# Mixture-of-experts stage of a two-layer decoder: the gathered token tile is turned by VectorE in 32x32 blocks instead of by TensorE

## The chip, the cores and the metric

The kernel runs as one program on one core of a Trainium2 chip. A core has five engines that run their own instruction streams and meet only at semaphores: TensorE (PE, matrix multiplies and transposes against an identity matrix), VectorE (DVE), ScalarE (ACT), GpSimd (POOL) and SyncE (SP). The metric is the device time of one execution in microseconds, here the median of three runs. All arithmetic of this kernel is in 32-bit floats.

## The reference

A decoder of two layers over 8 sequences of 256 tokens with 512 features. The part that the change touches is the feed-forward block of the first layer, a mixture of 8 experts of which each token uses two:

```
logits = h @ router_w.T                      # 2048 tokens, 8 experts
vals, idx = lax.top_k(softmax(logits), 2)    # two experts per token
vals = vals / vals.sum(axis=-1, keepdims=True)
for each expert e:                           # gate_up_proj[e] is 704 x 512, down_proj[e] 512 x 352
    gate, up = split(h @ gup.T, 2)           # 352 columns each
    y = silu(gate) * up @ dp.T
    out += combine[:, e] * y
x = layernorm(x + out)
```

Before it stand a differential attention and a long convolution, behind it a causal attention, a cross attention and a shared-key attention, each with its layer norm.

## The kernel before, in words

The program is a row of stages with a barrier between them: `front_stage`, `long_conv_stage`, `middle_stage`, `experts_stage`, `tail_stage`. The middle stage computes the routing and sorts the 4096 (token, expert) pairs into 39 tiles (`TILES`) of 128 slots, so that every tile belongs to one expert. It leaves in SBUF the number of the expert of each tile (`tile_expert`), the token of each slot (`tokens`), all weights of the experts (`gu`, `down`), and the first tile already turned (`xT_first`). It also starts the gathers of tiles 0 and 1 into the two buffers `xg`.

`experts_stage` goes over the tiles. For tile s:

- GpSimd gathers the 128 token rows of 512 features from memory into `xg[s % 2]` (L1604), slots on partitions. It may start once tile s - 2 has been turned (`x_turned`).
- The rows must be turned so that features are on partitions. TensorE does this with 4 transposes of 128x128 into the PSUM tile `xT_ps` (`turn_x`, L1618), and VectorE copies that to the single SBUF buffer `xT` (`take_x`, L1700), which signals `xT_taken`.
- TensorE multiplies: `gate` (4 products of 352 columns, summed in PSUM) and `up` (4 more), both at L1623. Each is preceded by `expert(s)` (L1610), with which TensorE's sequencer reads the number of the expert from SBUF into a register, and by a little register arithmetic for the address of the weights. In the instruction stream the waits of `gate` stand ahead of that read.
- ScalarE applies silu to the gate half (L1674), VectorE multiplies it with the up half (`product`, L1705, into `hid`).
- TensorE turns `hid` (3 transposes, L1642), ScalarE copies it (L1689, L1691), TensorE multiplies with the down weights (`down`, 3 products of 512 columns, L1651), VectorE copies the result to `y` (L1717), and ScalarE's queue stores it (L1678).

The order is written out by hand. TensorE's order in a turn of the loop is gate(s+1), turn hid(s), up(s+1), turn_x(s+2), down(s). VectorE's order is product(s+1), take_x(s+2), copy of y(s). The products of gate and up, the PSUM tile of y, `silu`, `hid` and `xg` have two buffers each; `xT` has one.

In the records a 32-bit product appears as two MATMUL instructions, a 32-bit transpose as one.

Of the kernel before, what the change touches and what calls it, by code (L numbers as in the profile page):

```python
# [13 lines left out]
P = 128  # L14
B = 8
# [3 lines left out]
NC = D // P  # L19
# [183 lines left out]
STRIP = 32  # L203
# [723 lines left out]
E_, HID = 8, 352  # L927
HC = [(0, P), (P, P), (2 * P, HID - 2 * P)]
PICKS = 2
TILES = PICKS * B * NT + E_ - 1  # L930
KB4 = 4 * D * NT
AT_CTX = 0
# [221 lines left out]
def ctx_stores(b):  # L1154

    return sum(2 if n >= EARLY else 1 for n in range(b % 2, b, 2))
# [420 lines left out]
def experts_stage(nc, consts, mid, region, x_in, y_slots, early, early_loaded, w_tail):  # L1577


    with ExitStack() as ctx:  # L1580
        st = Stage(nc, ctx, "moe")
        at = AT_SMALL + 320 + 4 * D
        xT = mid.xT
        hT = region.at("moe_hT", at + 2048, [P, 3, P])
        y = [region.at(f"moe_y{p}", at + 3584 + 2048 * p, [P, D]) for p in range(2)]
        silu = region.at("moe_silu", AT_CTX + 2 * KB4, [P, 2, HID])
        hid = region.at("moe_hid", AT_CTX + 2 * KB4 + 2816, [P, 2, HID])
        xg, wgu, wd, gathered = mid.xg, mid.gu, mid.down, mid.gathered
        gu_ps = st.ps("gu_ps", [P, 2, 2, 512])
        xT_ps = st.ps("xT_ps", [P, 512])  # L1590
        hT_ps = st.ps("hT_ps", [P, 512])
        y_ps = st.ps("y_ps", [P, 2, 512])
        y_stored = mid.y_stored
        sem = {n: st.sem(n) for n in (
            "x_turned", "xT_taken", "gate_ready", "up_ready", "silu_ready", "hid_ready", "h_turned", "hT_taken", "y_ready", "y_taken")}

        with nc.Block() as block:
            @block.gpsimd
            def _(pool):
                for s in range(2, TILES):  # L1600
                    p = s % 2
                    if s > 2:
                        pool.wait_ge(sem["x_turned"], s - 2)
                    pool.indirect_dma_start(out=xg[p][:], out_offset=None, in_=x_in,  # L1604
                                            in_offset=bass.IndirectOffsetOnAxis(ap=mid.tokens[:, s:s + 1], axis=0)).then_inc(gathered[p], 16)

            @block.tensor
            def _(pe):
                def expert(s):
                    return pe.value_load(mid.tile_expert[0:1, s:s + 1], min_val=0, max_val=E_ - 1)  # L1610

                def turn_x(s):
                    p = s % 2
                    pe.wait_ge(gathered[p], 16 * (s // 2) + 16)
                    if s > 1:
                        pe.wait_ge(sem["xT_taken"], s - 1)
                    for c in range(NC):
                        ins = pe.transpose(xT_ps[:, c * P:(c + 1) * P], xg[p][:, c * P:(c + 1) * P], consts["ident"][:])  # L1618
                    ins.then_inc(sem["x_turned"], 1)

                def project(s, h, e):
                    for c in range(NC):
                        ins = pe.matmul(gu_ps[:, s % 2, h, 0:HID], (xT if s else mid.xT_first)[:, c, :], wgu[c][:, e, h * HID:(h + 1) * HID],  # L1623
                                        start=c == 0, stop=c == NC - 1)
                    return ins

                def gate(s):
                    if s:
                        pe.wait_ge(sem["xT_taken"], s)
                    if s >= 2:  # L1630
                        pe.wait_ge(sem["hid_ready"], s - 1)
                    project(s, 0, expert(s)).then_inc(sem["gate_ready"], 1)

                def up(s):
                    project(s, 1, expert(s)).then_inc(sem["up_ready"], 1)

                def turn_hid(s):
                    pe.wait_ge(sem["hid_ready"], s + 1)
                    if s:
                        pe.wait_ge(sem["hT_taken"], s)  # L1640
                    for n, (lo, w) in enumerate(HC):
                        ins = pe.transpose(hT_ps[0:w, n * P:(n + 1) * P], hid[:, s % 2, lo:lo + w], consts["ident"][:])  # L1642
                    ins.then_inc(sem["h_turned"], 1)

                def down(s):
                    e = expert(s)
                    pe.wait_ge(sem["hT_taken"], s + 1)
                    if s >= 2:
                        pe.wait_ge(sem["y_taken"], s - 1)
                    for n, (lo, w) in enumerate(HC):  # L1650
                        ins = pe.matmul(y_ps[:, s % 2, :], hT[0:w, n, :], wd[n][0:w, e, :], start=n == 0, stop=n == 2)  # L1651
                    ins.then_inc(sem["y_ready"], 1)

                pe.wait_ge(mid.first_half, 16 * 7)
                gate(0)
                turn_x(1)
                up(0)
                for s in range(TILES):
                    if s + 1 == HALVES[1][0]:
                        pe.wait_ge(mid.second_half, 16 * 6)  # L1660
                    if s + 1 < TILES:
                        gate(s + 1)
                    turn_hid(s)
                    if s + 1 < TILES:
                        up(s + 1)
                    if s + 2 < TILES:
                        turn_x(s + 2)
                    down(s)

            @block.scalar  # L1670
            def _(act):
                def swish(s):
                    act.wait_ge(sem["gate_ready"], s + 1)
                    act.activation(silu[:, s % 2, :], gu_ps[:, s % 2, 0, 0:HID], ACT.Silu).then_inc(sem["silu_ready"], 1)  # L1674

                def store(s):
                    act.wait_ge(sem["y_taken"], s + 1)
                    act.dma_start(y_slots[s * P:(s + 1) * P, :], y[s % 2][:]).then_inc(y_stored[s % 2], 16)  # L1678

                for p in range(2):  # L1680
                    act.wait_ge(mid.ctx_stored[p], 16 * ctx_stores(B - 2 + p))
                for k in early:
                    act.dma_start(early[k][:], w_tail[k].rearrange("(c p) e -> p c e", p=P)).then_inc(early_loaded[k], 16)
                swish(0)
                for s in range(TILES):
                    if s + 1 < TILES:
                        swish(s + 1)
                    act.wait_ge(sem["h_turned"], s + 1)
                    act.copy(hT[:, 0:2, :], hT_ps[:, 0:2 * P].rearrange("p (k n) -> p k n", n=P))  # L1689
                    w = HC[2][1]  # L1690
                    act.copy(hT[0:w, 2, :], hT_ps[0:w, 2 * P:3 * P]).then_inc(sem["hT_taken"], 1)  # L1691
                    if s:
                        store(s - 1)
                store(TILES - 1)

            @block.vector
            def _(dve):
                def take_x(s):
                    dve.wait_ge(sem["x_turned"], s)
                    dve.tensor_copy(xT[:], xT_ps[:].rearrange("p (c n) -> p c n", n=P)).then_inc(sem["xT_taken"], 1)  # L1700

                def product(s):
                    dve.wait_ge(sem["silu_ready"], s + 1)
                    dve.wait_ge(sem["up_ready"], s + 1)
                    dve.tensor_tensor(hid[:, s % 2, :], gu_ps[:, s % 2, 1, 0:HID], silu[:, s % 2, :], ALU.mult).then_inc(sem["hid_ready"], 1)  # L1705

                take_x(1)
                product(0)
                for s in range(TILES):
                    if s + 1 < TILES:  # L1710
                        product(s + 1)
                    if s + 2 < TILES:
                        take_x(s + 2)
                    dve.wait_ge(sem["y_ready"], s + 1)
                    if s >= 2:
                        dve.wait_ge(y_stored[s % 2], 16 * (s // 2))
                    dve.tensor_copy(y[s % 2][:], y_ps[:, s % 2, :]).then_inc(sem["y_taken"], 1)  # L1717
# [1271 lines left out]
```

## Times and profile before

| what | value |
|---|---|
| median of 3 runs | 2129.55 us (2128.58 to 2134.21) |
| span of the profiled execution, first to last instruction | 2127.3 us |
| the median less that span | 2.25 us |
| PE busy | 2057.7 us, 97% |
| DVE busy | 1128.4 us, 53% |
| ACT busy, POOL busy | 518.8 us, 580.5 us |
| mean granted TensorE clock | 0.992 of full speed |
| experts stage, from its first product to the last product of down | about 860 to 1178 us |

The profiled execution has no time of its own beside its span, so the span stands for it. Busy time is the time in which an engine executed instructions; waiting, register and semaphore instructions are not in it. The rows below use the names PEld for TensorE's weight loads, which overlap its products, and PEldq for instructions of TensorE's sequencer (register reads and arithmetic). A row of the timeline has start, duration, engine, line, operation, output<-inputs, and how often; in brackets the idle time of the engine before it and what ended that. Durations of neighbouring rows on one engine can overlap, so that the distance between starts is what an instruction costs in a row of instructions.

### The profile page before, as it was taken

The page shows a single profiled execution, that of the slowest core. Times are in us where ns is not written, and L with a number is a line of the kernel's source. Part 1 is how long each engine was busy: PE and PEld are TensorE (multiplying, and loading weights), DVE is VectorE, ACT ScalarE, POOL GpSimd, SP SyncE. Part 2 cuts the span into 40 slices and gives each one's busy share as a digit, 9 for nine tenths or more (in the row PEclk, how much of TensorE's full clock was granted, in tenths as well). Part 3 has the DMA queues.
Part 4 walks back from the last instruction along what each step waited for, and adds up shares of the span by engine and source line. Part 5 has one row for each costly group of instructions (what it writes and reads, how often), then busy time and mean ns, then how long its engine had stood idle before and what let it go on. Part 6 is the DMA issues. An engine that isn't in the chain of part 4 may idle for free. (4 is left out here: it accounts for less than half of the span.)

```text
span 2127.3 us, 32323 instructions
## 1 busy us (share of the span) xinstructions
PE 2057.7 (97%) x13439; PEld 1194.6 (56%) x13439; DVE 1128.4 (53%) x1731; ACT 518.8 (24%) x791; POOL 580.5 (27%) x548
## 2 busy tenths in 40 slices
PE   7899999999999999999999999999999999999996
PEld 5444444334444557556566655766666666666664
DVE  2567777567777744122222334364646464736567
ACT  2445555440000121101011122122222222222211
POOL 2222222128999600111110312022222222121122
PEclk9999999999999999999999999999999999999998
DMA  5101111205111147321211602100010101000000
GB/s 161 48 1 55 55 56 45 87 38 210 40 43 44 35 156 277 126 65 65 65 65 55 222 3 99 50 31 21 17 44 1 60 1 41 1 31 12 1 11 21
DMA packets 66237, 130.81 MB, mean 61 GB/s; under 512 B 6480, under 2 KB 19920, under 8 KB 66096
## 3 DMA queue, kind: packets, MB, share of 16 engines
q1 hardware_dynamic: 45968, 77.49, 11.1%
q10 hardware_dynamic: 14448, 32.64, 4.3%
q0 software_dynamic: 5680, 18.62, 3.0%
q8 instruction: 111, 1.82, 0.4%
q14 instruction: 30, 0.25, 0.0%
HBM read 97.40 MB, written 41.81 MB: 65 GB/s over the span
## 5 line engine op out<-in xcount | busy, mean ns | idle before, releaser
L1033 PE MATMUL conv_conv<-kv,toep 128*128 128x512 f32 x576 | 247.6, 592 | 0.3 <-POOL kv L1067 0.3
L2615 DVE RECIPROCAL tail_inv<-tail_ring 128x256 f32<-128x256 f32 x63 | 110.7, 1757 | 188.8 <-PE tail_ring L1935 188.3
L1623 PE MATMUL moe_gu_ps<-gu,xT_tile 128*128 x608 | 192.4, 459 | 0.0
L1033 PEld LDWEIGHTS conv_conv<-kv,toep 128*128 128x128 f32 x576 | 109.4, 190 | 139.0 <-issue 129.6
L1067 POOL TENSOR_TENSOR kv<-vT,cT 128x512 f32<-128x512 f32 x128 | 147.0, 1172 | 15.8 <-PE conv_conv L1033 12.0
L2302 POOL TENSOR_TENSOR tail_rstd_x<-tail_rstd_x,const_minus_half 128x2 f32<-128x2 f32 x31 | 21.8, 702 | 469.6 <-DVE tail_rstd_x L2577 469.6
L1623 PEld LDWEIGHTS moe_gu_ps<-gu,xT_tile 128*128 128x128 f32 x608 | 112.3, 190 | 66.5 <-issue 17.8
L2310 POOL TENSOR_SCALAR_AFFINE_SELECT tail_expT<-tail_expT 128x1024 f32<-128x1024 f32 x64 | 71.5, 1119 | 242.1 <-ACT tail_expT L2394 242.0
L2603 DVE TENSOR_REDUCE tail_negtop<-tail_scores 128x4 f32<-128x1024 f32 x64 | 78.2, 1221 | 95.6 <-PE tail_scores L1886 95.4
L594 POOL TENSOR_SCALAR_AFFINE_SELECT front_expT<-front_expT 128x2048 f32<-128x2048 f32 x32 | 64.3, 2008 | 199.1 <-ACT front_expT L649 199.1
L1604 POOL DMA_INDIRECT xg<-x_after,tokens x37 | 35.0, 947 | 282.3 <-PE moe_xT_ps L1618 255.2
L1705 DVE TENSOR_TENSOR moe_hid<-moe_gu_ps,moe_silu 128x352 f32<-128x352 f32 x39 | 20.5, 525 | 170.7 <-PE moe_gu_ps L1623 170.7
L649 ACT ACTIVATE front_expT<-front_scores 128x2048 f32<-128x2048 f32 x48 | 90.1, 1878 | 78.3 <-PE front_scores L367 78.3
L1651 PE MATMUL moe_y_ps<-down,moe_hT 128*128 (+1 forms) x234 | 107.1, 593 | 0.7 <-ACT moe_hT L1691 0.7
L2394 ACT ACTIVATE tail_expT<-tail_scores 128x1536 f32<-128x1536 f32 x63 | 91.4, 1451 | 64.8 <-PE tail_scores L1912 64.8
L1674 ACT ACTIVATE moe_silu<-moe_gu_ps 128x352 f32<-128x352 f32 x39 | 18.1, 464 | 270.2 <-PE moe_gu_ps L1623 270.2
L770 DVE TENSOR_REDUCE front_negtop<-front_scores 128x8 f32<-128x2048 f32 x32 | 73.2, 2288 | 18.6 <-PE front_scores L335 18.4
L2315 POOL TENSOR_TENSOR tail_expT<-tail_expT 128x512 f32<-128x512 f32 x60 | 76.7, 1279 | 5.0
L1089 ACT COPY both<-conv_conv 128x512 f32<-128x512 f32 x32 | 18.7, 586 | 229.9 <-PE conv_conv L1033 211.0
L1717 DVE COPY moe_y<-moe_y_ps 128x512 f32<-128x512 f32 x39 | 27.0, 692 | 72.7 <-PE moe_y_ps L1651 72.7
L198 PE MATMUL tail_ring<-tail_gk,tail_xT 128*128 128x416 f32 (+1 forms) x256 | 63.4, 399 | 1.5 <-ACT tail_xT L2376 1.5
L1651 PEld LDWEIGHTS moe_y_ps<-down,moe_hT 128*128 128x128 f32 (+1 forms) x234 | 41.6, 191 | 38.5 <-issue 38.3
(394 smaller groups left out, 3912.2 us busy)
## 6 DMA issues: line engine op xcount, KB each, us to landing
toep<-toeplitz SPq DMA_DIRECT2D x32, 320.0 KB, 2.9
y_slots<-moe_y ACTq DMA_DIRECT2D x39, 256.0 KB, 2.0
gu<-in_L_ffn_gate_up_proj SPq DMA_DIRECT2D x5, 1408.0 KB, 12.5
toeplitz<-filt_rows SPq DMA_DIRECT2D x8, 768.0 KB
front_e<-in_ctx SPq DMA_DIRECT2D x8, 512.0 KB, 4.7
toeplitz<-filt_rows SPq DMA_DIRECT2D x16, 256.0 KB
x_after<-x SPq DMA_DIRECT2D x8, 512.0 KB, 5.0
tail_x<-x_after SPq DMA_DIRECT2D x8, 512.0 KB, 3.7
```

The costliest lines, as they stand in the source:

```text
L594: pool.affine_select(out=tile, in_=tile, compare_op=ALU.is_ge, fill=0.0, base=0, pattern=[[0, 16], [1, P]], channel_multiplier=-1).then_in ...
L649: act.activation(exp_buf(b, n)[:].rearrange("p g j q -> p g (j q)"), scores[:], ACT.Exp).then_inc(quads.drained_sem(key), 1)
L770: ins = dve.tensor_reduce(negtop[:, 1, n].rearrange("p (g a) -> p g a", a=2), scores[:].rearrange("p g (a k) -> p g a k", a=2), AX_X, ALU. ...
L1033: ins = pe.matmul(bank, toep[p][:, mat * P:(mat + 1) * P], kv[p][:, c].rearrange("p b j i -> p (b j i)"), start=n == 0, stop=n == len(PART ...
L1067: pool.tensor_tensor(kv[p][:, c], tokens_of(c, h), context_of(c, h, 3), ALU.mult).then_inc(kv_ready, 1)
L1623: ins = pe.matmul(gu_ps[:, s % 2, h, 0:HID], (xT if s else mid.xT_first)[:, c, :], wgu[c][:, e, h * HID:(h + 1) * HID], start=c == 0, stop ...
L1651: ins = pe.matmul(y_ps[:, s % 2, :], hT[0:w, n, :], wd[n][0:w, e, :], start=n == 0, stop=n == 2)
L2310: pool.affine_select(out=diagonal, in_=diagonal, compare_op=ALU.is_ge, fill=0.0, base=0, pattern=[[0, 8], [1, P]], channel_multiplier=-1). ...
L2315: pool.tensor_tensor(e[:, 3], e[:, 0], e[:, 2], ALU.add).then_inc(masked[kind], 1)
L2394: act.activation(exp_buf(kind, b, c)[:, 0:3].rearrange("p n g q -> p g n q"), quads.tile(key)[:, :, 0:3 * P].rearrange("p g (n q) -> p g n ...
L2603: dve.tensor_reduce(negtop[:, 1, heads_of(c)], scores[:, :, 0:S], AX_X, ALU.max, negate=True)
L2615: link.after(dve.reciprocal(inv[c % 2][:], bank[:, S:2 * S]))
```

## The change

The four transposes by TensorE and VectorE's copy out of PSUM are gone, and so are the PSUM tile `xT_ps` and the semaphore `xT_taken`. VectorE now turns the tile itself, SBUF to SBUF. One instruction reads 32 slots (one strip of 32 partitions) by 4 blocks of 32 features and writes 32 features (one strip of partitions) by 4 blocks of 32 slots; 16 of them, for all pairs of strips, make up a tile. The buffer `xT` now has two halves, by the parity of the tile. `x_turned` is raised by the last of the 16, and both `gate(s)` and the gather of tile s + 2 wait for it. From tile 3 on, the turns of tile s wait in addition for `up(s - 2)`, the last reader of the same half. The turns of tile 1, which write to an area that a store of the middle stage still reads, wait for that store (`ctx_stored`).

```diff
@@ -1580,19 +1580,18 @@
     with ExitStack() as ctx:
         st = Stage(nc, ctx, "moe")
         at = AT_SMALL + 320 + 4 * D
-        xT = mid.xT
+        xT = [mid.xT, region.at("moe_xT1", AT_CTX + 2 * KB4 + 5632, [P, NC, P])]
         hT = region.at("moe_hT", at + 2048, [P, 3, P])
         y = [region.at(f"moe_y{p}", at + 3584 + 2048 * p, [P, D]) for p in range(2)]
         silu = region.at("moe_silu", AT_CTX + 2 * KB4, [P, 2, HID])
         hid = region.at("moe_hid", AT_CTX + 2 * KB4 + 2816, [P, 2, HID])
         xg, wgu, wd, gathered = mid.xg, mid.gu, mid.down, mid.gathered
         gu_ps = st.ps("gu_ps", [P, 2, 2, 512])
-        xT_ps = st.ps("xT_ps", [P, 512])
         hT_ps = st.ps("hT_ps", [P, 512])
         y_ps = st.ps("y_ps", [P, 2, 512])
         y_stored = mid.y_stored
         sem = {n: st.sem(n) for n in (
-            "x_turned", "xT_taken", "gate_ready", "up_ready", "silu_ready", "hid_ready", "h_turned", "hT_taken", "y_ready", "y_taken")}
+            "x_turned", "gate_ready", "up_ready", "silu_ready", "hid_ready", "h_turned", "hT_taken", "y_ready", "y_taken")}
 
         with nc.Block() as block:
             @block.gpsimd
@@ -1609,24 +1608,15 @@
                 def expert(s):
                     return pe.value_load(mid.tile_expert[0:1, s:s + 1], min_val=0, max_val=E_ - 1)
 
-                def turn_x(s):
-                    p = s % 2
-                    pe.wait_ge(gathered[p], 16 * (s // 2) + 16)
-                    if s > 1:
-                        pe.wait_ge(sem["xT_taken"], s - 1)
-                    for c in range(NC):
-                        ins = pe.transpose(xT_ps[:, c * P:(c + 1) * P], xg[p][:, c * P:(c + 1) * P], consts["ident"][:])
-                    ins.then_inc(sem["x_turned"], 1)
-
                 def project(s, h, e):
                     for c in range(NC):
-                        ins = pe.matmul(gu_ps[:, s % 2, h, 0:HID], (xT if s else mid.xT_first)[:, c, :], wgu[c][:, e, h * HID:(h + 1) * HID],
+                        ins = pe.matmul(gu_ps[:, s % 2, h, 0:HID], (xT[s % 2] if s else mid.xT_first)[:, c, :], wgu[c][:, e, h * HID:(h + 1) * HID],
                                         start=c == 0, stop=c == NC - 1)
                     return ins
 
                 def gate(s):
                     if s:
-                        pe.wait_ge(sem["xT_taken"], s)
+                        pe.wait_ge(sem["x_turned"], s)
                     if s >= 2:
                         pe.wait_ge(sem["hid_ready"], s - 1)
                     project(s, 0, expert(s)).then_inc(sem["gate_ready"], 1)
@@ -1653,7 +1643,6 @@
 
                 pe.wait_ge(mid.first_half, 16 * 7)
                 gate(0)
-                turn_x(1)
                 up(0)
                 for s in range(TILES):
                     if s + 1 == HALVES[1][0]:
@@ -1663,8 +1652,6 @@
                     turn_hid(s)
                     if s + 1 < TILES:
                         up(s + 1)
-                    if s + 2 < TILES:
-                        turn_x(s + 2)
                     down(s)
 
             @block.scalar
@@ -1695,22 +1682,30 @@
 
             @block.vector
             def _(dve):
-                def take_x(s):
-                    dve.wait_ge(sem["x_turned"], s)
-                    dve.tensor_copy(xT[:], xT_ps[:].rearrange("p (c n) -> p c n", n=P)).then_inc(sem["xT_taken"], 1)
+                def turn_x(s):
+                    dve.wait_ge(gathered[s % 2], 16 * (s // 2) + 16)
+                    if s > 2:
+                        dve.wait_ge(sem["up_ready"], s - 1)
+                    rows = xg[s % 2][:].rearrange("p (c d) -> p c d", d=P)
+                    for a in range(4):
+                        for k in range(4):
+                            lane, tokens = slice(STRIP * k, STRIP * (k + 1)), slice(STRIP * a, STRIP * (a + 1))
+                            ins = dve.transpose(xT[s % 2][lane, :, tokens], rows[tokens, :, lane])
+                    ins.then_inc(sem["x_turned"], 1)
 
                 def product(s):
                     dve.wait_ge(sem["silu_ready"], s + 1)
                     dve.wait_ge(sem["up_ready"], s + 1)
                     dve.tensor_tensor(hid[:, s % 2, :], gu_ps[:, s % 2, 1, 0:HID], silu[:, s % 2, :], ALU.mult).then_inc(sem["hid_ready"], 1)
 
-                take_x(1)
+                dve.wait_ge(mid.ctx_stored[1], 16 * ctx_stores(B - 1))
+                turn_x(1)
                 product(0)
                 for s in range(TILES):
                     if s + 1 < TILES:
                         product(s + 1)
                     if s + 2 < TILES:
-                        take_x(s + 2)
+                        turn_x(s + 2)
                     dve.wait_ge(sem["y_ready"], s + 1)
                     if s >= 2:
                         dve.wait_ge(y_stored[s % 2], 16 * (s // 2))
```

VectorE in two turns of the loop, before and after. `moe_hid` is the product, `xT_tile` and `moe_xT` are the two halves of the turned tile, `moe_y` is the result tile.

```order
L1705 TENSOR_TENSOR moe_hid<-moe_gu_ps,moe_silu 128x352 [waits moe_up_ready,moe_silu_ready]
L1700 COPY xT_tile<-moe_xT_ps 128x512 [waits moe_x_turned]
L1717 COPY moe_y_7466<-moe_y_ps 128x512 [waits mid_y_stored1,moe_y_ready]
L1705 TENSOR_TENSOR moe_hid<-moe_gu_ps,moe_silu 128x352 [waits moe_up_ready,moe_silu_ready]
L1700 COPY xT_tile<-moe_xT_ps 128x512 [waits moe_x_turned]
```

```order
L1699 TENSOR_TENSOR moe_hid<-moe_gu_ps,moe_silu 128x352 [waits moe_up_ready,moe_silu_ready]
L1693 STREAM_TRANSPOSE xT_tile<-xg_75 32x4x32 [waits moe_up_ready,mid_gathered0]
L1693 STREAM_TRANSPOSE xT_tile<-xg_75 32x4x32 x15
L1712 COPY moe_y_7466<-moe_y_ps 128x512 [waits mid_y_stored0,moe_y_ready]
L1699 TENSOR_TENSOR moe_hid<-moe_gu_ps,moe_silu 128x352 [waits moe_up_ready,moe_silu_ready]
```

One copy of 512 columns has become 16 transposes of 32 partitions by 128 elements, at the same place behind the product and ahead of the copy of y.

TensorE from the end of one tile's up products to the start of the next tile's gate, before and after. The TENSOR_LOAD behind down is the read of the expert's number for the next gate.

```order
L1618 MATMUL moe_xT_ps<-const_ident,xg_75 128x128 [waits moe_xT_taken,mid_gathered0]
L1618 MATMUL moe_xT_ps<-const_ident,xg_75 128x128 x3
L1610 TENSOR_LOAD tile_expert
L1610 ISA x2
L1651 ISA [waits moe_hT_taken]
L1651 MATMUL moe_y_ps<-down_68,moe_hT 128x512
L1651 REGISTER_ALU
L1651 MATMUL moe_y_ps<-down_69,moe_hT 128x512
L1651 REGISTER_ALU
L1651 MATMUL moe_y_ps<-down_70,moe_hT 128x512
L1610 TENSOR_LOAD tile_expert [waits moe_hid_ready,moe_xT_taken]
```

```order
L1609 TENSOR_LOAD tile_expert
L1609 ISA x2
L1641 ISA [waits moe_hT_taken]
L1641 MATMUL moe_y_ps<-down_68,moe_hT 128x512
L1641 REGISTER_ALU
L1641 MATMUL moe_y_ps<-down_69,moe_hT 128x512
L1641 REGISTER_ALU
L1641 MATMUL moe_y_ps<-down_70,moe_hT 128x512
L1609 TENSOR_LOAD tile_expert [waits moe_hid_ready,moe_x_turned]
```

The transposes are gone from between up and down, and the read of the expert's number now waits for VectorE's last transpose instead of for its copy.

## Rows read from the trace of the kernel before

**Rows 1.** Page, part 1: busy time, share of the span, instructions.
```profile
PE 2057.7 (97%) x13439; PEld 1194.6 (56%) x13439; DVE 1128.4 (53%) x1731; ACT 518.8 (24%) x791; POOL 580.5 (27%) x548
```

**Rows 2.** Windows: us, busy PE, PEld, DVE, ACT, POOL (instructions), granted clock, DMA share, GB/s.
```profile
870.00:1170.00 300.00, 300.00 (x1079) 180.01 (x1078) 67.11 (x111) 33.56 (x114) 33.16 (x35) 1.00 0.19 63
```

**Rows 3.** Waits of PE from 858 to 1180: us in total, times, longest.
```profile
PE moe_gu_ps L1623 <- issue: 4.2, 1, 4.2
...
PE moe_y_ps L1651 <- ACT moe_hT L1691: 0.7, 1, 0.7
```

**Rows 4.** Timeline from 1001.69 to 1012.79, one tile and the next.
```profile
1001.69 0.60 PE L1618 MATMUL moe_xT_ps<-const_ident,xg 128*128 128x128 f32 x4
...
1001.96 0.53 DVE L1705 TENSOR_TENSOR moe_hid<-moe_gu_ps,moe_silu 128x352 f32<-128x352 f32 x1 [4.44 <-PE moe_gu_ps L1623]
...
1002.13 2.74 PE L1651 MATMUL moe_y_ps<-down,moe_hT 128*128 x6
1002.40 0.68 DVE L1700 COPY xT_tile<-moe_xT_ps 128x512 f32<-128x512 f32 x1
...
1002.57 0.95 POOL L1604 DMA_INDIRECT xg<-x_after,tokens  x1 [7.13 <-PE moe_xT_ps L1618]
...
1004.28 0.19 PEld L1623 LDWEIGHTS moe_gu_ps<-gu,xT_tile 128*128 128x128 f32 x1 [0.24 <-issue]
1004.71 2.53 PE L1623 MATMUL moe_gu_ps<-gu,xT_tile 128*128 x8
...
1012.79 2.53 PE L1623 MATMUL moe_gu_ps<-gu,xT_tile 128*128 x8
```

**Rows 5.** Lines L1610 and L1623 around 1003 to 1004.3: durations ns min/median/max, first and last start.
```profile
L1610 PEldq TENSOR_LOAD <-tile_expert x1: 300/300/300, 1003.1 to 1003.1; - x1
...
L1623 PEldq ALU_OP  x3: 32/32/32, 1003.9 to 1004.1; - x3
```

**Rows 6.** Timeline at 826: a weight load after a wait, and its product.
```profile
826.57 1.43 PEld L1338 LDWEIGHTS midl_ring<-marked,at_lane 128*128 128x128 bf16 x32 [0.44 <-DVE marked L1561]
826.79 1.34 PE L1338 MATMUL midl_ring<-marked,at_lane 128*128 128x78 bf16 x32
```

**Rows 7.** Groups of DVE, shapes apart: busy us, mean ns of one.
```profile
L2571 DVE BATCH_NORM_STATS2 tail_stats_x<-tail_x 128x6 f32<-128x512 f32 x62 | 39.9, 685 | 1.0
...
L2573 DVE MEMSET tail_pause<- 128x1 f32 x31 | 1.8, 59 | 0.0
...
L873 DVE COPY front_wq<-front_expT 128x1024 f32<-128x1024 f32 x1 | 0.7, 695 | 9.3 <-DMA front_expT<-in_L_attn_Wq 9.3
...
L1540 DVE TENSOR_REDUCE slot_f<-ranked 128x16 f32<-128x128 f32 x2 | 0.6, 286 | 0.1
```

**Rows 8.** Timeline of DVE: two linked instructions at 802, two independent ones at 1426.
```profile
801.96 0.29 DVE L1517 TENSOR_REDUCE which<-ranked 128x16 f32<-128x128 f32 x1
802.28 0.29 DVE L1518 TENSOR_TENSOR ind<-ranked,which 128x128 f32<-128x128 f32 x1
...
1426.04 1.29 DVE L2571 BATCH_NORM_STATS2 tail_stats_x<-tail_x 128x6 f32<-128x512 f32 x2
```

**Rows 9.** Timeline of PE: what it did first after two idle gaps.
```profile
395.49 1.98 PE L416 MATMUL front_ring<-front_wq,cT 128*128 128x512 f32 x4 [2.90 <-DMA front_wq<-in_L_xattn_wo]
860.37 2.31 PE L1623 MATMUL moe_gu_ps<-gu,xT_first 128*128 x5 [4.17 <-issue]
```

**Rows 10.** Windows around and behind these two gaps.
```profile
388.00:398.00 10.00, 6.86 (x58) 2.39 (x55) 6.17 (x11) 5.26 (x6) 3.23 (x2) 1.00 0.69 204
861.40:864.80 3.40, 3.40 (x9) 2.03 (x8) 0.00 (x0) 0.63 (x1) 0.00 (x0) 0.50 0.56 216
```

**Rows 11.** Timeline at 863.7, and the gathers' time to landing (tile xg).
```profile
863.75 0.39 ACTq L1683 DMA_DIRECT2D early_wq<-in_L_attn_w_qkv  x1
867.33 2.53 PE L1623 MATMUL moe_gu_ps<-gu,xT_tile 128*128 x8
...
DMA to landing us min/median/max: 3.1/3.4/8.8
```

## The prediction, made before the changed kernel had run

> **What bounds the kernel now.** I read first the busy shares, then the stage of the change by windows, then who waited there, then one tile in the timeline, and last the sequencer's own rows.
>
> The busy shares say TensorE: 97% of the span, VectorE 53% [rows 1]. In the experts stage it is sharper. Of the 300 us from 870 to 1170 TensorE is busy in all 300, VectorE in 67.1, at a granted clock of 1.00 [rows 2]. TensorE's waits in the whole stage are 4.2 us at its start and once 0.7 us [rows 3]. So here the time is the sum of TensorE's work, and taking work from it would pay, if nothing else becomes late.
>
> One tile takes 8.08 us: gate starts at 1004.71 and again at 1012.79 [rows 4]. The part to look at is the one from the end of up to the next gate, 1001.69 to 1004.71, 3.02 us. It holds the four transposes (1001.69 to 1002.13, 0.44 us) and down (to 1004.71, 2.58 us). The rest, gate, turn of hid and up, is 5.06 us.
>
> Beside it runs a chain that no wait shows, because it is just in time [rows 4, 5]. VectorE's product starts at 1001.96, its next instruction at 1002.40, and that copy ends at 1003.08. Then TensorE's sequencer reads the expert's number (TENSOR_LOAD at 1003.1), computes addresses (to 1004.1), and the gate's first weight load starts at 1004.28. That is 1.20 us from the end of VectorE's work to the weight load. The load comes 0.43 us ahead of its product, the distance of the down products, so neither side waits. The read stands behind the wait in the stream, so it can't run ahead.
>
> **The change, part by part.** Taken from TensorE: 38 times 0.44 us, 16.7 us. This is all that can be gained; everything else is what the replacement costs.
>
> Taken from VectorE: the copy, 0.68 us. Put in its place: 16 transposes, in the chain just described. They are behind the product, which waits for the end of up, and ahead of the next gate, which waits for the last of them. The only cover is down, 2.58 us. Counted from the end of up (1001.69 in the old trace), the next gate's first product comes after
>
> 0.27 (to the product's start) + 0.44 (to the next instruction) + the 16 turns + 1.20 (sequencer) + 0.22 (weight load to product after a wait [rows 6]) = 2.13 us + the turns.
>
> Against the 3.02 us of before, the change is even at 0.89 us of turns, 0.056 us each.
>
> What does one turn cost? The trace has no transpose on VectorE, so I bound it. One handles 128 elements per partition, and that partitions are few doesn't shorten a row. Instructions over 128 elements take 0.286 us, over 512 elements 0.685 us [rows 7]; the difference is 1.04 ns an element and 0.15 us fixed. Independent neighbours overlap: two of 0.685 take 1.29 together, so the second costs 0.60, some 0.08 less than its duration [rows 8]. Linked neighbours don't: they start 0.32 apart at a duration of 0.29 [rows 8].
>
> - Lowest: a plain copy at its best rate, 1024 elements in 0.695 us [rows 7]. At half a nanosecond an element and the same 0.16 fixed, 128 take 0.23 us, overlapped 0.145. Sixteen: 15 x 0.145 + 0.23 = 2.4 us.
> - Overlapped at the ordinary rate: 15 x 0.20 + 0.29 = 3.3 us.
> - One after the other: 16 x 0.31 = 5.0 us, 0.31 lying between the duration and the linked distance.
> - Highest: the same with 2 ns an element, 16 x 0.44 = 7.0 us.
>
> I take one after the other. Its nearest row is the linked pair, with the same 128 elements: each turn writes another strip of partitions than the one before, and no row of VectorE in this trace, all of them over 128 partitions from the first on, shows two such instructions overlapping.
>
> The Trainium skill has a rule on this ("VectorE: DVE Perf Modes", section "Two Vector instructions with no wait between them"): a Vector instruction whose input or output begins in another group of 32 partitions than that of the one before it is held until all earlier ones are finished. The 16 turns change the output's group each time, so by the rule all would be held, and the sum below would stand; without it the overlapped case (first rival) would. This trace can't show it. The same page (section "The three transpose paths") gives 311 ns for a 128-column bf16 transpose; by that 16 would be 4.98 us.
>
> So the gate comes 2.13 + 4.96 = 7.09 us after up instead of 3.02, the tile takes 4.07 us more, about 12.15. This holds for 37 gates, those of tiles 2 to 38: 150.6 us. Tile 1 has its own start: its turns wait for the store that ScalarE also waits for until 863.75 [rows 11]. From there 4.96 + 1.42 give the gate at 870.1 instead of 867.33, 2.8 us.
>
> Edits at nothing: the gathers are started by the last turn instead of by TensorE, and have a whole tile more than their 0.95 + 3.4 us [rows 4, 11] before they are needed; their cover of some 12 us doesn't go away. The copy of y now stands behind 5 us of turns, but its PSUM tile and buffer have a twin, and the wait of down for it reaches two tiles back. The added wait for `up(s - 2)` is met when the product before it has run. Product, hid and ScalarE's work lie under gate as before.
>
> Last, the clock. After the chain TensorE will have stood idle for 7.09 - 2.58, some 4.4 us, in each tile. In this trace it stood idle 4.17 us before 860.37 [rows 9], and from 861.4 to 864.8 the granted clock was 0.50, 1.2 GHz instead of 2.4 [rows 10]. After 2.90 us idle at 395.49 it stayed at 1.00 [rows 9, 10]. 4.4 us is nearer to the first, so I expect a low stretch after each gap. It costs at most half its 3.4 us, 1.7 us, if gate and up fill it, and less if part of it falls into the gap. I take 1.5 us: 37 x 1.5 = 55.5 us. Bounds: 0 and 63.
>
> Sum: 150.6 + 2.8 + 55.5 = 209 us. The span would be 2127.3 + 209 = 2336; with the 2.25 us by which the median stands above this span, 2338.5 us.
>
> **Rivals.**
>
> *Overlapped turns.* Each costs 0.20 us, 3.3 us in all; for it speaks that all independent neighbours in the trace overlap. The gate comes 5.42 us after up, 2.40 us late: 88.8 us, and 1 us at the start. The gap is then 2.7 us, near the one after which the clock stayed; I charge half of the clock's 55.5. 2129.55 + 89.8 + 28 = 2247 us. At the lowest price, 2.4 us, and no fall of the clock it would be 1.5 x 37 = 55.5 us, 2185 us.
>
> *One after the other, but the clock holds.* 2129.55 + 153.4 = 2283 us. For it: TensorE still works over half the time, and single gaps of 2.90 us passed.
>
> *Dearer turns.* At 0.44 us each the gate is 6.15 us late: 227.6 + 5 + 55.5, 2418 us. Against it: 1.04 ns an element holds for every ordinary row.
>
> *Faster than before.* The one mechanism is that the turns fit under down: 16 in under 0.89 us. Then the chain is hidden as now and TensorE's 16.7 us come off: 2113 us. It decides at 0.056 us a turn. A memset of one element takes 0.059 [rows 7], so this needs turns cheaper than the cheapest instruction there is. That the change doesn't do what it says can't be: TensorE's transposes are gone from its stream and the turns stand in VectorE's.
>
> **How the numbers follow.** One after the other with a falling clock 0.53, with a steady clock 0.15, overlapped 0.22, dearer 0.07, faster 0.02, the remaining 0.01 for no change. The time is that of the first, 2338 us, its own range 2315 to 2365. Leaving out the dearest, the cheapest and the faster ends, the range is 2228 to 2385. About 0.3%, 6.4 us, is what a measurement of this kernel can tell from no change; all cases but the last two are far above it: faster 0.02, same 0.01, slower 0.97.
>
> **What would show it.** Turns starting 0.3 us apart (0.2 in the rival) and about 5 us for sixteen; the sequencer's read of the expert's number right behind the last turn, and 1.4 us from there to the gate's product; the gate's wait on VectorE in all 37 tiles, 4.4 us each; a tile of 12 to 13.7 us in the timeline instead of 8.08; the granted clock over 870 to 1170 clearly below 1. TensorE busy under the whole stage would prove me wrong, and so would turns that run ahead of the product.

## The result, and the profile after

| | median us | runs | ratio to before (95%) |
|---|---|---|---|
| before | 2129.07 | 4 | 1 |
| changed | 2339.28 | 4 (2338.54 to 2341.39) | 1.0987 (1.0968 to 1.1006) |

The change costs 210 us. The prediction was 2338 us, range 2228 to 2385. The total came out nearly exact, but two of its terms were off by some 16 us each, in opposite directions.

The busy shares of the changed kernel (page, part 1), to be read against [rows 1]:

```profile
PE 2124.5 (91%) x13287; PEld 1217.1 (52%) x13287; DVE 1284.6 (55%) x2301; ACT 521.4 (22%) x791; POOL 580.0 (25%) x548
```

TensorE has 152 instructions less and is busy 67 us more: so each instruction takes longer on average, and the cause is its clock, shown below. VectorE is busy 156 us more for 570 more instructions.

The experts stage by windows, columns as in [rows 2]. It now lasts from about 863 to 1389 us (1386.17 + 2.84, the last down):

```profile
870.00:1370.00 500.00, 360.70 (x925) 198.56 (x924) 217.79 (x658) 35.55 (x111) 34.00 (x36) 0.84 0.12 40
```

TensorE, which was busy in all of the stage, is busy in 72% of it, and its mean granted clock fell from 1.00 to 0.84. The waits of the changed kernel from 870 to 1380 (us in total, times, longest) name the cause of the idle part, which in [rows 3] doesn't exist:

```profile
PE moe_gu_ps L1613 <- DVE moe_xT L1693: 70.6, 19, 3.9
PE moe_gu_ps L1613 <- DVE xT_tile L1693: 68.6, 18, 3.9
PE moe_gu_ps L1613 <- issue: 3.9, 1, 3.9
```

These are all 38 gates of tiles 1 to 38, the one put down to "issue" among them. Tile 1's wait is 2.05 us; the other 37 wait 141 us together, 3.8 us each. One tile at full clock in the timeline, which answers to [rows 4]:

```profile
878.04 2.74 PE L1641 MATMUL moe_y_ps<-down,moe_hT 128*128 x6
...
878.31 0.52 DVE L1699 TENSOR_TENSOR moe_hid<-moe_gu_ps,moe_silu 128x352 f32<-128x352 f32 x1 [5.84 <-PE moe_gu_ps L1613]
...
878.75 5.03 DVE L1693 STREAM_TRANSPOSE xT_tile<-xg 32x128 f32<-32x128 f32 x16
...
883.82 0.69 DVE L1712 COPY moe_y<-moe_y_ps 128x512 f32<-128x512 f32 x1
884.05 0.94 POOL L1603 DMA_INDIRECT xg<-x_after,tokens  x1 [10.92 <-DVE xT_tile L1693]
...
884.66 0.30 PEld L1613 LDWEIGHTS moe_gu_ps<-gu,xT_tile 128*128 128x128 f32 x2 [4.71 <-issue]
884.67 0.56 PE L1613 MATMUL moe_gu_ps<-gu,xT_tile 128*128 x1 [3.89 <-DVE xT_tile L1693]
```

Up ends and down begins at 878.04; the product follows after 0.27 us, the 16 turns after another 0.44, they take 5.03, and the gate's first product comes 0.89 us behind them (0.79 in most tiles). From up to gate these are 6.63 us where [rows 4] have 3.02. The line of the turns alone (durations in ns, minimum, median, maximum):

```profile
L1693 DVE STREAM_TRANSPOSE moe_xT<-xg x304: 289/303/308, 866.9 to 1361.1; 32x128 f32<-32x128 f32 x152
```

Last, the clock in the tiles after 1006.9, by windows, and the gate of the second of them in the timeline:

```profile
1006.90:1008.20 1.30, 1.29 (x5) 0.87 (x6) 0.00 (x0) 0.00 (x0) 0.42 (x1) 1.00 0.11 19
1008.30:1011.60 3.30, 3.30 (x9) 2.06 (x8) 0.00 (x0) 0.68 (x2) 0.00 (x0) 0.50 0.20 70
1011.70:1018.40 6.70, 4.80 (x14) 2.28 (x12) 4.21 (x14) 0.22 (x2) 0.00 (x0) 1.00 0.10 39
1018.50:1025.20 6.70, 4.90 (x9) 2.80 (x10) 1.66 (x5) 0.00 (x0) 0.94 (x1) 0.50 0.14 39
```
```profile
1020.30 5.06 PE L1613 MATMUL moe_gu_ps<-gu,xT_tile 128*128 x8 [3.80 <-DVE xT_tile L1693]
```

In two of three tiles the clock falls to half 0.7 to 1.4 us after the gate has begun, for about 3.4 us. In every third tile it is low for 6.8 us and falls some 1.8 us before the gate (here at about 1018.5, the gate at 1020.30), so that 1.8 us of the low stretch lie in the idle gap and 5.0 on work. The distance of the gates is therefore two of about 13.4 us and one of 14.2, on average 13.64 (from the first gate behind the turns, at 884.67, over 36 distances).

### The profile page after: what moved, and what is told of

It reads as the page before. It is cut to its first block and busy times, and to the rows that moved or that the text cites. A ratio compares the mean times of both kernels' runs of the same rounds, so it can differ in the third digit from the quotient of the medians.

```text
span 2338.3 us, 32589 instructions
## 1 busy us (share of the span) xinstructions
PE 2124.5 (91%) x13287; PEld 1217.1 (52%) x13287; DVE 1284.6 (55%) x2301; ACT 521.4 (22%) x791; POOL 580.0 (25%) x548
## 5 line engine op out<-in xcount | busy, mean ns | idle before, releaser
L1613 PE MATMUL moe_gu_ps<-gu,xT_tile 128*128 x304 | 131.4, 589 | 72.5 <-DVE xT_tile L1693 68.6
L1613 PE MATMUL moe_gu_ps<-gu,moe_xT 128*128 x304 | 128.8, 579 | 70.6 <-DVE moe_xT L1693 70.6
L1613 PEld LDWEIGHTS moe_gu_ps<-gu,xT_tile 128*128 128x128 f32 x304 | 69.6, 241 | 123.0 <-issue 106.7
L1613 PEld LDWEIGHTS moe_gu_ps<-gu,moe_xT 128*128 128x128 f32 x304 | 68.4, 237 | 119.9 <-issue 103.1
L1693 DVE STREAM_TRANSPOSE moe_xT<-xg 32x128 f32<-32x128 f32 x304 | 91.8, 302 | 17.5 <-DMA ctx_o<-ctxo 13.6
L1693 DVE STREAM_TRANSPOSE xT_tile<-xg 32x128 f32<-32x128 f32 x304 | 91.8, 302 | 3.9
```

Of the source, the lines that this page charges most:

```text
L1613: ins = pe.matmul(gu_ps[:, s % 2, h, 0:HID], (xT[s % 2] if s else mid.xT_first)[:, c, :], wgu[c][:, e, h * HID:(h + 1) * HID], start=c == ...
L1693: ins = dve.transpose(xT[s % 2][lane, :, tokens], rows[tokens, :, lane])
```

## The experiments

The theory: VectorE's turns stand where only down covers them; each waits for the end of the one before because the strips change; and the idle gap costs a second time through the clock. The rivals: VectorE or SBUF is the limit wherever the turns stand; a transpose never starts before the one ahead of it has ended, whatever the strips; the clock records don't matter to the time. Ratios are to the kernel before, run on the same chip.

**e1: the turns one tile earlier.**

```diff
                 turn_x(1)
                 product(0)
+                turn_x(2)
                 for s in range(TILES):
                     if s + 1 < TILES:
                         product(s + 1)
-                    if s + 2 < TILES:
-                        turn_x(s + 2)
+                    if s + 3 < TILES:
+                        turn_x(s + 3)
```

> The 16 turns stay on VectorE but are issued one tile earlier: after the product of tile s+1 come the turns of tile s+3 instead of s+2. Theory (the place in the order is what costs, since only down, 2.6 us, lies between the product and the gate that needs the turns): the turns have a whole tile of cover, VectorE's work per tile (0.44 + 5.04 + 0.69 = 6.2 us) fits under TensorE's 8.08 - 0.44 = 7.64 us, no wait is left, the granted clock stays at 1.00, and the stage is 38 x 0.44 us shorter than before the change: about 2115 us, some 2.5 us of it for a later start of tile 1. Rival (VectorE or its access to SBUF beside the gathers is the limit, wherever the turns stand): no better than 2129 us, with waits of TensorE on the turns left.

Measured: 2116.55 us, ratio 0.9944 (0.9930 to 0.9957), faster than before the change. The timeline of TensorE in it, and the window of the stage:

```profile
1001.03 2.53 PE L1613 MATMUL moe_gu_ps<-gu,xT_tile 128*128 x8
1003.39 0.49 PE L1632 MATMUL moe_hT_ps<-const_ident,moe_hid 128*128 128x128 f32 x3
1003.72 2.53 PE L1613 MATMUL moe_gu_ps<-gu,xT_tile 128*128 x8
1006.09 2.74 PE L1641 MATMUL moe_y_ps<-down,moe_hT 128*128 x6
1008.67 0.76 PE L1613 MATMUL moe_gu_ps<-gu,moe_xT 128*128 x2
```
```profile
870.00:1150.00 280.00, 278.99 (x915) 163.18 (x916) 220.16 (x666) 32.77 (x111) 34.01 (x36) 1.00 0.21 67
```

A tile takes 1008.67 - 1001.03 = 7.64 us, just the 8.08 less 0.44 of the prediction's first term, at a clock of 1.00. TensorE waits for nothing from 880 to 1150. The same 608 turns are done, VectorE is busy in 79% of the stage, and this costs nothing. So the loss is the place in the order, and the rival "VectorE is the limit" is out.

**e2: TensorE's idle gap filled.**

```diff
+        fill_ps = st.ps("fill_ps", [P, 512])
...
                     down(s)
+                    if s + 2 < TILES:
+                        for n in range(4):
+                            pe.matmul(fill_ps[:], consts["ident"][:], wd[0][:, 0, :], start=True, stop=True)
```

> The changed kernel with 4 products of 512 columns added on TensorE behind each down (results unused), which fill most of the 3.8 us in which it stands idle (4 x 0.86 us = 3.4 us), and end before the turns do. Theory (the idle gap costs twice, once itself and once by the lower clock behind it): the granted clock stays at 1.00 over the stage, a tile takes 11.6 us (5.06 of TensorE's work, and 0.27 + 0.44 + 5.04 + 0.8 from up to gate), 37 x 3.52 = 130 us over before: about 2262 us, 77 us faster than the changed kernel although it does more work. Rival (the clock records mean little, and the 13.6 us of a tile are the wait and the turns alone): 2339 us.

Measured: 2265.75 us, ratio 1.0641 (1.0624 to 1.0657). Its stage and two neighbouring gates:

```profile
880.00:1280.00 400.00, 387.27 (x1127) 201.25 (x1126) 204.52 (x618) 30.12 (x102) 32.10 (x34) 1.00 0.14 45
```
```profile
1001.74 2.63 PE L1614 MATMUL moe_gu_ps<-gu,xT_tile 128*128 x8 [0.37 <-issue]
...
1009.48 3.60 PE L1659 MATMUL moe_fill_ps<-down,const_ident 128*128 128x512 f32 x8
```

With 37 x 4 products more, the kernel is 74 us faster than the changed one, and the clock is 1.00. The turns of a tile start 11.7 us after those of the tile before instead of 13.6 (means of 37 distances), and the gate's product comes 0.79 us behind the last turn in most tiles, as in the changed kernel, so the filler doesn't hold it back. This shows the clock's share of the loss directly: about 74 of the 210 us by the medians, 71 by the profiled spans (2338.3 - 2267.2).

**e3: half of the turns.** The second 64 slots of a tile are left out (zeros in their place).

```diff
+                for half in xT:
+                    dve.memset(half[:], 0.0).then_inc(sem["cleared"], 1)
+                dve.wait_ge(sem["cleared"], 2)
...
-                    for a in range(4):
+                    for a in range(2):
```

> The changed kernel with 8 of the 16 turns of each tile left out (only the first 64 slots are turned; the rest of the buffer is zero). Theory (each turn costs 0.316 us on the path, and the clock falls only after long gaps): the turns take 2.52 us, the gate comes 0.27 + 0.44 + 2.52 + 0.8 = 4.03 us after up, the gap is some 1.4 us, the clock stays at 1.00, a tile takes 9.09 us: 37 x 1.01 = 37 us over before, about 2168 us. Rival (the clock falls after any gap that returns every tile): up to 2 us more in each tile, about 2243 us.

Measured: 2170.72 us, ratio 1.0205 (1.0189 to 1.0221). In its trace 8 turns take 2.50 us and 36 gates wait 46.4 us in all, 1.3 us each:

```profile
PE moe_gu_ps L1613 <- DVE moe_xT L1693: 23.4, 18, 1.6
PE moe_gu_ps L1613 <- DVE xT_tile L1693: 23.0, 18, 1.4
```
```profile
880.00:1180.00 300.00, 257.41 (x814) 142.31 (x812) 116.78 (x330) 28.42 (x97) 30.83 (x33) 1.00 0.18 57
```

A gap of 1.3 us in each tile leaves the clock at 1.00. That the gap returns every tile doesn't bring the clock down; a short gap costs only itself.

**e4: the turns within one strip.** Each block lands in the strip it came from, so the tile is turned wrongly; the 16 instructions have the same size.

```diff
-                            lane, tokens = slice(STRIP * k, STRIP * (k + 1)), slice(STRIP * a, STRIP * (a + 1))
-                            ins = dve.transpose(xT[s % 2][lane, :, tokens], rows[tokens, :, lane])
+                            same, cols = slice(STRIP * a, STRIP * (a + 1)), slice(STRIP * k, STRIP * (k + 1))
+                            ins = dve.transpose(xT[s % 2][same, :, cols], rows[same, :, cols])
```

> The changed kernel with each turn writing the strip of partitions that it reads, four in a row on the same strip (16 turns of the same size; the blocks land in the wrong places). Theory (a turn waits for the end of the one before because the strips change from one to the next): 12 of the 15 distances fall from 0.316 to about 0.21 us, the turns take 3.8 us instead of 5.04, the gap about 2.6 us; 2213 us if the clock then stays, up to 2290 us if it falls. Rival (a transpose always empties its array before the next begins, whatever the strips): distances stay at 0.316 us and the time at 2339 us.

Measured: 2213.64 us, ratio 1.0402 (1.0386 to 1.0418). Its line of the turns, one tile of them in the timeline, four single ones of that tile, its waits, and its stage by windows:

```profile
L1693 DVE STREAM_TRANSPOSE moe_xT<-xg x304: 256/260/309, 866.1 to 1240.0; 32x128 f32<-32x128 f32 x152
```
```profile
1001.01 3.57 DVE L1693 STREAM_TRANSPOSE xT_tile<-xg 32x128 f32<-32x128 f32 x16
```
```profile
1001.23 0.26 DVE L1693 STREAM_TRANSPOSE xT_tile<-xg 32x128 f32<-32x128 f32 x1
1001.42 0.26 DVE L1693 STREAM_TRANSPOSE xT_tile<-xg 32x128 f32<-32x128 f32 x1
1001.62 0.26 DVE L1693 STREAM_TRANSPOSE xT_tile<-xg 32x128 f32<-32x128 f32 x1
1001.89 0.30 DVE L1693 STREAM_TRANSPOSE xT_tile<-xg 32x128 f32<-32x128 f32 x1
```
```profile
PE moe_gu_ps L1613 <- DVE moe_xT L1693: 43.4, 19, 2.5
PE moe_gu_ps L1613 <- DVE xT_tile L1693: 42.2, 18, 2.5
```
```profile
880.00:1230.00 350.00, 270.38 (x850) 149.80 (x850) 158.26 (x612) 30.12 (x102) 32.12 (x34) 1.00 0.16 52
```

The 16 take 3.57 us instead of 5.03. On one strip the turns start 0.19 us apart (0.235 behind the first of the four), before the one ahead, of 0.26 us, has ended. The first turn on the next strip, here at 1001.89, starts 0.27 us after the one before it, just when that has ended, and takes 0.30 us itself. The changed kernel has 0.316 from start to start at a duration of 0.303 everywhere. So transposes do overlap, and a change of the strips holds the next one until the one before has ended. One thing stays open: in the change every pair of neighbours also has at least one turn that writes another strip than it reads, and no run has such turns in a row on unchanged strips. Whether crossing alone would hold a turn is not shown.

```profile
880.70 4.32 PE L1613 MATMUL moe_gu_ps<-gu,xT_tile 128*128 x8 [2.32 <-DVE xT_tile L1693]
...
881.00:884.30 3.30, 3.30 (x7) 1.83 (x6) 0.00 (x0) 0.00 (x0) 0.13 (x1) 0.50 0.29 79
```

The gap of 2.3 us left the clock at full speed in all but the first of the 37 tiles, whose gate and clock are the two lines above; with 3.8 us it fell in every one. Which property of the gaps decides, their length or how much of a tile they take, these runs don't separate: both grow from e3 over e4 to the change.

**e5 and e6: VectorE's part of the old chain made longer,** in the kernel before the change, with instructions whose results nothing reads. Both also wait once, ahead of the first copy, for the store that still reads the area of `spare`. e5:

```diff
+        spare = region.at("moe_spare", AT_CTX + 2 * KB4 + 5632, [P, 2, P])
...
                 def take_x(s):
+                    wide = consts["octets"][:].unsqueeze(1).to_broadcast([P, 2, P])
+                    dve.tensor_tensor(spare[:], wide, wide, ALU.mult)
...
+                dve.wait_ge(mid.ctx_stored[1], 16 * ctx_stores(B - 1))
                 take_x(1)
```

> The kernel before, with one more VectorE instruction over 256 elements (not used by anything) between the product and the copy of the turned tile; by the rates of its neighbours it puts the copy 0.34 us later. The prediction held that this chain is just in time, with 1.20 us from the copy's end to the gate's weight load: then every gate comes 0.34 us later, 37 x 0.34 = 12.6 us, 2140 us. The changed kernel's trace shows 0.8 us from VectorE's end to the gate's product instead, which leaves some 0.4 us of slack: then no change, 2128 us.

Measured: 2129.19 us, ratio 1.0001 (0.9991 to 1.0012): no change, although its timeline shows the copy 0.34 us later.

```profile
1001.38 0.41 DVE L1701 TENSOR_TENSOR moe_spare<-const_octets 128x256 f32<-128x256 f32 x1
1001.72 0.68 DVE L1703 COPY xT_tile<-moe_xT_ps 128x512 f32<-128x512 f32 x1
```

e6 has five in place of the one:

```diff
                 def take_x(s):
+                    for n in range(5):
+                        dve.tensor_tensor(spare[:, n], consts["octets"][:], consts["octets"][:], ALU.mult)
```

> As the one before, but with five more instructions of 128 elements, 5 x 0.205 = 1.03 us. Just in time: 37 x 1.03 = 38 us, 2166 us. With 0.4 us of slack: 37 x 0.6 = 23 us, 2151 us. The two runs together give the slack.

Measured: 2139.46 us, ratio 1.0050 (1.0035 to 1.0065), less than either expectation. From its timeline, VectorE and TensorE:

```profile
1007.12 1.09 DVE L1701 TENSOR_TENSOR moe_spare<-const_octets 128x128 f32<-128x128 f32 x5
1008.13 0.68 DVE L1703 COPY xT_tile<-moe_xT_ps 128x512 f32<-128x512 f32 x1
```
```profile
1001.24 2.63 PE L1624 MATMUL moe_gu_ps<-gu,xT_tile 128*128 x8
...
1006.84 2.74 PE L1652 MATMUL moe_y_ps<-down,moe_hT 128*128 x6
1009.59 1.74 PE L1624 MATMUL moe_gu_ps<-gu,xT_tile 128*128 x5
```

The copy comes 1.01 us later (1008.13 - 1007.12), and this tile takes 8.35 us (1009.59 - 1001.24), 0.27 more. Of these, 0.17 are the gate's later start (2.75 us behind down's instead of 2.58 in [rows 4]), and 0.10 that the gate itself now takes 2.63 us instead of 2.53. So the old chain had 1.01 - 0.17 = 0.84 us of slack. From the copy's end at 1008.81 to the gate's product there are 0.78 us, where [rows 4] have 1.63 (1003.08 to 1004.71); the difference is 0.85, the same slack.

**e7: the loops over the strips exchanged.**

```diff
-                    for a in range(4):
-                        for k in range(4):
+                    for k in range(4):
+                        for a in range(4):
```

> The changed kernel with the two loops over the strips exchanged: four turns in a row now write the same strip and read different ones, where the change has four in a row read the same strip and write different ones. If a change of either strip holds a turn back until the one before has ended, the distances stay at 0.316 us, 2339 us. If only a change of the written strip counts, 12 of 15 distances fall to about 0.19 us as in the run on the same strips, the turns take 3.6 us, 2214 us.

Measured: 2335.57 us, one run, and the same durations:

```profile
L1693 DVE STREAM_TRANSPOSE moe_xT<-xg x304: 289/303/308, 860.7 to 1356.4; 32x128 f32<-32x128 f32 x152
```

The distances stay at 0.316 us. With the strip that is read changing from turn to turn, the next turn is held back as much as with the strip that is written. In any order of the 16 blocks of a true transpose at least one of the two changes at each step, so by these two runs no order escapes it.

**e8: e1 with the two buffers exchanged,** so that the turns of tile 1 needn't wait for a store.

```diff
-        xT = [mid.xT, region.at("moe_xT1", AT_CTX + 2 * KB4 + 5632, [P, NC, P])]
+        xT = [region.at("moe_xT1", AT_CTX + 2 * KB4 + 5632, [P, NC, P]), mid.xT]
...
-                dve.wait_ge(mid.ctx_stored[1], 16 * ctx_stores(B - 1))
                 turn_x(1)
+                dve.wait_ge(mid.ctx_stored[1], 16 * ctx_stores(B - 1))
                 product(0)
```

> The turns issued one tile earlier, as in the first experiment, with the two buffers of the turned tile exchanged, so that tile 1 goes to a buffer that no store still reads, and its turns don't wait for that store (865.2 us in the first experiment's trace). They can then begin at the stage's start, about 860.5, end at 865.5, and be in time for the gate of tile 1, which came 1.4 us late there. Expected: 1.4 to 3 us less than the first experiment, about 2114 us, hardly above what a comparison can tell. If the start of the stage is bound by its first products alone, no change.

Measured: 2111.93 us, ratio 0.9929 (0.9914 to 0.9944). Its timeline shows the gate of tile 1 right behind the products of tile 0:

```profile
857.07 6.64 PE L1613 MATMUL moe_gu_ps<-gu,xT_first 128*128 x16 [3.82 <-issue]
857.76 2.52 DVE L1693 STREAM_TRANSPOSE xT_tile<-xg 32x128 f32<-32x128 f32 x8
...
863.55 2.53 PE L1613 MATMUL moe_gu_ps<-gu,xT_tile 128*128 x8
```

The same place in e1:

```profile
861.85 7.73 PE L1613 MATMUL moe_gu_ps<-gu,xT_first 128*128 x16 [3.98 <-issue]
...
871.01 2.63 PE L1613 MATMUL moe_gu_ps<-gu,moe_xT 128*128 x8 [1.44 <-DVE moe_xT L1693]
```

From the stage's first product to the gate of tile 1 it is 6.48 us in e8 and 9.16 in e1. Of the 2.7 us between them 1.44 are the wait that the edit removes; most of the rest is that tile 0's products ran longer at the lower clock in e1. The other 4.8 us of the 7.5 between the two profiled spans arose before the stage, in code that is the same in both: over the ten profiled runs of this document the stage's first product comes anywhere from 857.07 to 863.46. The intervals of e1 and e8 overlap, so that e8 beats e1 is likely and not proved; that it beats the kernel before is clear. In the stage itself, from the first product to the end of the last down, e8 takes 300.92 us where the kernel before took 317.65. It is the fastest version run.

## Why the prediction was right, step by step

- **What bounded the kernel, and the 16.7 us to be gained:** right. e1 gets a tile of 7.64 us, and the stage of e8 is 16.7 us shorter than before the change.
- **The place of the turns in the order:** right, and the main thing. The gates of all 37 tiles wait, as forecast.
- **Price of a turn:** 0.31 us forecast, 0.316 from start to start, 5.03 us for 16 against 4.96. The duration is 0.303. The rule of the Trainium skill that was cited ("VectorE: DVE Perf Modes", section "Two Vector instructions with no wait between them") separated the forecast from its first rival, and the runs agree with it: 0.19 us apart on one strip, and at a change of strips a start just when the one before has ended (0.27 us in e4, 0.316 in the change and e7). The price itself came from the linked pair of [rows 8]. The kernel whose turns do overlap, e4, measured 2213.64 us; the rival had 2247.
- **"This chain is just in time":** wrong. The working read 1.20 us between the copy's end and the weight load as time that the sequencer needs, because load and address work happened to end together. But the gate's first weight load needs the address of the first weights only. In the changed kernel the sequencer's rows show it (the two lines around 1006 to 1007.2, columns as in [rows 5]):

```profile
L1609 PEldq TENSOR_LOAD <-tile_expert x1: 297/297/297, 1006.1 to 1006.1; - x1
```
```profile
L1613 PEldq ALU_OP  x3: 32/32/32, 1006.9 to 1007.2; - x3
L1613 PEld LDWEIGHTS moe_gu_ps<-gu,moe_xT x2: 187/188/189, 1006.9 to 1007.0; 128*128 128x128 f32 x2
```

  The weight load at 1006.9 runs beside the remaining address work instead of behind it, and the product starts with it (884.66 and 884.67 above) where the sum had 0.22 us between the two. From VectorE's end to the gate's product it is 0.8 us where the sum had 1.20 + 0.22. e5 and e6 show that the old chain had some 0.84 us of slack. On the other side, the eight products of a gate that has waited take 2.63 instead of 2.53 us (e2 and e6 above), which no term had. The term "4.07 us a tile" should have been 0.27 + 0.44 + 5.04 + 0.80 + 0.10 - 3.02 = 3.63: 134 us instead of 150.6.
- **The clock:** the mechanism was right, its size too small. The fall was expected from the one gap of 4.17 us in [rows 9, 10], at 1.5 us a tile. The gaps became 3.8 us, not some 4.4 (and the working's 7.09 - 2.58 is 4.51), and the clock fell in all 37 tiles. The tile is 13.64 us long and would be 8.08 + 3.63 = 11.71 at full clock, which is just the tile of e2; so the clock costs 1.93 us a tile, 71 us in 37. The medians of e2 put it at 74, its profiled span at 71. What was missed is the longer low stretch in every third tile: half of the low time that lies on work is (3.4 + 3.4 + 5.0) / 3 / 2 = 2.0 us a tile.
- **Start of the stage:** 2.8 us forecast. The gate of tile 1 comes at 872.88 instead of 867.33, 5.5 us later, of which 3.1 are already there at the stage's first product (863.45 against 860.37). They arose in code that the change doesn't touch and lie within the scatter told at e8. The change itself costs 2.5 us here.
- **Sum:** a tile is 13.64 - 8.08 = 5.56 us longer, some 205.5 us in 37, which e2 splits into 134 for the wait and 71 for the clock. With 2.5 for the start and 3.1 from before the stage that is 211 us, the difference of the spans, 2338.3 - 2127.3. The forecast's 151 + 55.5 + 3 = 209 hit it because one term was 16 us too high and the other 16 too low. The range would have held either way; the closeness is luck.
- **Edits at nothing:** right. The gathers are never waited for, and neither the copy of y nor the added wait shows among the waits.

## What to carry to other kernels

Before work is moved from the engine that bounds a stage to one with spare time, look not at its share of busy time but at the place in its order: what must be finished before it, and how much of the busy engine's work lies between that and the next use. Here VectorE was busy in 22% of the stage and the move still cost 10%, while the same work issued one tile earlier gained 0.6 to 0.7%. A wait put on TensorE is to be priced with the clock that it may lose behind it, which was about a third of the bill; and a sequencer's distance in a trace in which nobody waits is an upper bound, not a cost.

## What the runs showed of the hardware

- A VectorE transpose of 32 partitions by 128 elements takes 0.26 us and is followed after 0.19 us if it reads and writes one strip and the next one does the same (e4). At a change of either strip the next one starts when it has ended: in the change and in e7 each takes 0.30 us and the next starts 0.316 us after it.
- Gaps of 1.3 us (e3) and 2.3 us (e4, but for its first tile) left TensorE's granted clock at 1.00; gaps of 3.8 us in each tile brought it to 0.50 for a third of the stage.
- An unused product on TensorE can pay: e2 does 148 products more and is 74 us faster than the same kernel without them.
- A transpose against the identity on TensorE costs 0.44 us a tile of 128x512 and a copy; VectorE's 16 turns cost 5.03 us of an engine that had the time.
